# Linear attention merged with the third feed-forward: sums first in VectorE's pass, two TensorE groups moved up by one pass

## What is computed

```python
x = x + _L2_xattn_ref(_layernorm(x, axis=-1), ctx_4096, ctx_4096)
x = x + _L2_ffn_ref(_layernorm(x, axis=-1), L2_ffn_router_w, L2_ffn_A, L2_ffn_B)
...
# _L2_xattn_ref: linear attention
qh = jax.nn.softmax(qh, axis=3)
kh = jax.nn.softmax(kh, axis=1)
kvs = jnp.einsum('bnhd,bnhe->bhde', kh, vh)
out = jnp.einsum('bnhd,bhde->bnhe', qh, kvs)
# _L2_ffn_ref: top 2 of 4 experts of rank 16, gates from the logits
logits = flat @ router_w.T
topk_vals, topk_idx = jax.lax.top_k(logits, TOP_K)
gates = jax.nn.softmax(sparse, axis=-1)
mid = jnp.einsum('tf,erf->ter', flat, A)
all_deltas = jnp.einsum('ter,eor->teo', mid, B) * LORA_SCALE
delta = jnp.einsum('te,teo->to', gates, all_deltas)
```

## Time and profile before

| what | value |
|---|---|
| three runs | 1657.16, 1661.85, 5148.23 us |
| their median | 1661.85 us |
| profiled execution, time / span | 1659.5 / 1657.8 us |
| granted clock, mean of the span | 0.964 |
| busy: PE, DVE, ACT, POOL | 93%, 64%, 50%, 20% |
| the merged stage (first L929 to first L1006) | 1378.0 to 1501.5 us |

### The profile page before, as it was taken

One profiled execution on the slowest core, in us unless ns is written; L12 is line 12 of the kernel. 1 busy time (PEld: TensorE's weight loads), 2 busy tenths in 40 slices (PEclk: granted clock), 3 DMA queues, 4 the chain that ended last, 5 costly groups with the idle time before them and its releaser, 6 DMA issues.

```text
span 1657.8 us, 27915 instructions
## 1 busy us (share of the span) xinstructions
PE 1544.3 (93%) x9690; PEld 1345.1 (81%) x9690; DVE 1064.4 (64%) x2585; ACT 820.7 (50%) x2869; POOL 336.9 (20%) x353
## 2 busy tenths in 40 slices
PE   6999999999999989889999999999999997767988
PEld 5898999999999978778888888888888776655766
DVE  6566556655655687756666666666666876754664
ACT  4556445554545553355555555555555414425540
POOL 4102101110101021222222223122222213313110
PEclk9999999999999999999999999999999997868989
DMA  5101010100001001101010101010100001100001
GB/s 199 31 26 57 9 51 27 39 27 26 26 27 39 27 28 48 39 26 39 26 39 26 39 26 43 22 64 24 42 30 4 30 4 51 61 1 20 33 4 51
DMA packets 13710, 59.43 MB, mean 36 GB/s; under 512 B 2131, under 2 KB 3155, under 8 KB 8454
## 3 DMA queue, kind: packets, MB, share of 16 engines
q1 hardware_dynamic: 13574, 57.67, 9.9%
HBM read 55.57 MB, written 2.10 MB: 35 GB/s over the span
## 4 chain that ended last, share of the span: by engine, by line
PE 51%; issue 29%; DVE 11%; POOL 4%; ACT 3%; DMA 1%; POOLq 0%; SPq 0%; ACTq 0%; DVEq 0%
PE psY L772 12%; PE psQ L697 8%; PE psKV L717 7%; PE psSO L760 2%; PE psSO L666 2%; PE psQ L682 2%; POOL wo L438 2%; PE psQ L1044 1%; PE psTP L682 1%; DVE wq L1515 1%; PE psSO L667 1%; PE psTP L727 1%; PE psKV L1006 1%; PE psKV L641 1%; PE psTP L745 1%
## 5 line engine op out<-in xcount | busy, mean ns | idle before, releaser
L772 PE MATMUL psY<-wo,oT 128*128 128x512 f32 x1536 | 384.7, 399 | 1.9 <-DVE oT L1515 1.3
L772 PEld LDWEIGHTS psY<-wo,oT 128*128 128x128 f32 x1536 | 278.4, 188 | 66.0 <-POOL wo L438 2.3
L697 PE MATMUL psQ<-wq,hT 128*128 128x512 f32 x768 | 212.2, 414 | 0.3 <-DVE wq L1515 0.3
L438 POOL TENSOR_TENSOR wo<-stage_o,wo 128x512 fp32r<-128x512 f32 (+2 forms) x72 | 93.7, 1331 | 322.9 <-ACT wo L1108 322.9
L697 PEld LDWEIGHTS psQ<-wq,hT 128*128 128x128 f32 x768 | 137.9, 193 | 24.6 <-DVE wq L1515 1.2
L539 POOL TENSOR_TENSOR rms<-ms_eps,minus_half 128x5 f32<-128x5 f32 x64 | 74.7, 1167 | 390.8 <-DVE ms_eps L1678 390.8
L1177 ACT ACTIVATE prob<-s_sb,neg_mx 128x64 f32<-128x64 f32 x256 | 86.1, 337 | 110.0 <-DVE neg_mx L1665 110.0
L1180 ACT ACTIVATE prob<-wide,neg_mx 128x128 f32<-128x128 f32 x256 | 99.7, 391 | 73.7 <-DVE neg_mx L1665 73.6
L1108 ACT ACTIVATE pT<-psTP 128x512 fp32r<-128x512 f32 (+1 forms) x128 | 62.3, 486 | 131.1 <-PE psTP L745 131.1
L717 PEld LDWEIGHTS psKV<-wkv,arena 128*128 128x128 f32 x768 | 99.4, 190 | 19.8 <-DVE kT L1515 15.7
L1515 DVE TENSOR_TENSOR pT<-psTP,pT 128x512 fp32r<-128x512 f32 (+1 forms) x128 | 70.7, 552 | 65.9 <-ACT pT L1108 65.3
(11 more groups left out here) (287 smaller groups left out, 3290.4 us busy)
## 6 DMA issues: line engine op xcount, KB each, us to landing
stage_q<-in_wq SPq DMA_DIRECT2D x16, 1024.0 KB, 5.3
stage_o<-in_wo SPq DMA_DIRECT2D x16, 1024.0 KB, 4.9
stage_kv<-in_wkv SPq DMA_DIRECT2D x12, 512.0 KB, 3.6
stage_q<-in_ctx SPq DMA_DIRECT2D x16, 256.0 KB, 4.2
stage_o<-in_ctxT SPq DMA_DIRECT2D x2, 1024.0 KB, 6.9
stage_q<-in_base SPq DMA_DIRECT2D x2, 1024.0 KB, 5.1
out<-x_res SPq DMA_DIRECT2D x8, 256.0 KB, 2.0
x_res<-in_x SPq DMA_DIRECT2D x1, 1536.0 KB, 13.2
```

Source lines behind the costliest of these rows:

```text
L438: g.tensor_tensor(dst[LO], stage, dst[HI].bitcast(f32), ALU.subtract).then_inc(ld[what + "_lo"], 1)
L697: m = mm(psQ[:], lat(xl, k, n), wq[:, wl, k, :], start=k == 0 and i == 0, stop=k == KT - 1 and i == 2)
L772: m = mm(psY[:], oT[:, ol, h, :], wo[:, wl, h, :], start=h == 0 and i == 0, stop=h == HQ - 1 and i == 2)
```

## The change

Nothing is added to or taken from the computation. Tile lags stay as they are for most steps; what changes is the order within each engine's pass. On TensorE the pass is now: exponentials' transposes of t, LN-5 transposes of t-4, gate product of e, query product of t-2, key-value product of tile t (was t-1), hidden transpose of e, result transposes of t-2 (was t-3), experts of e, LN-6 transposes of e-2. On VectorE the attention sum of t-3 comes first, then `ln_lo(6, e-3)` (was e-2, at the pass's end), the key-value matrix, statistics, the exponentials' low half, and only then the experts' sum and the gates; y, `ln_lo(5)`, `hidden_lo` and the row maxima follow. ScalarE and GpSimd are reordered to match, with `ln_hi(6, e-3)` at the head of ScalarE's pass and the context's exponential and `hidden_hi` near its end. The hidden transpose moves to the gate product's bank, psS. There is one pass more, 15 in place of 14 for t (to NT + 7), which holds only the last halves of LN 6.

```diff
-    psE, psK2, psH = psSO[:, 1], psSO[:, 2, 0:2 * P], psSO[:, 2, 2 * P:3 * P]
+    psE, psK2, psH = psSO[:, 1], psSO[:, 2, 0:2 * P], psSO[:, 0, 2 * P:3 * P]
# GpSimd: ln_rstd(6, e - 1) and ln_nmr(6, e - 1, ...) moved from the head of the pass to behind q_lo
# TensorE
-            if 0 <= e < NT:
-                gate_product(f, e)
-            if 0 <= t - 1 < NT:
-                pe.wait_ge(s["eT_lo"], t)
-                need(pe, s["kvs"], t - 1)
...
-            if 0 <= t - 3 < NT:
-                u = t - 3
-                pe.wait_ge(s["y"], u + 1)
...
-            if 0 <= e < NT:
-                pe.wait_ge(s["kvs"], min(t, NT))
-                hidden_transpose(f, e)
...
                 ln_transpose(5, t - 4, free)
+            if 0 <= e < NT:
+                need(pe, FS["hidT_lo"], f.done + e)
+                gate_product(f, e)
...
                 m.then_inc(s["out"], 1)
+            if t < NT:
+                pe.wait_ge(s["eT_lo"], t + 1)
+                need(pe, s["kvs"], t)
...
+            if 0 <= e < NT:
+                hidden_transpose(f, e)
+            if 0 <= t - 2 < NT:
+                u = t - 2
+                pe.wait_ge(s["y"], u + 1)
...
             if 0 <= e < NT:
                 experts(f, e)
...
-        for t in range(3, NT + 7):
+        for t in range(3, NT + 8):
# ScalarE
-            if 0 <= e < NT:
-                gate_exp(f, e)
+            if 0 <= e - 3 < NT:
+                ln_hi(6, e - 3)
...
-            if 0 <= e < NT:
-                hidden_hi(f, e)
...
-            if t + 1 < NT:
-                ctx_exp(t + 1)
+            if 0 <= t - 4 < NT:
+                ln_hi(5, t - 4)
+            if 0 <= e < NT:
+                gate_exp(f, e)
...
-            if 0 <= e - 2 < NT:
-                ln_hi(6, e - 2)
+            if t + 1 < NT:
+                ctx_exp(t + 1)
+            if 0 <= e < NT:
+                hidden_hi(f, e)
             if 0 <= e - 1 < NT:
                 ln_norm_act(6, e - 1)
# VectorE
-            if 0 <= e - 1 < NT:
-                experts_add(f, e - 1)
-            if 0 <= e < NT:
-                gates(f, e, e - 1 if e > 0 else None, 6)
...
             if 0 <= t - 3 < NT:
                 dve.wait_ge(s["y_tr"], t - 2)
                 V.tensor_tensor(x[:, t - 3], x[:, t - 3], psY[:], ALU.add).then_inc(s["x_add"], 1)
+            if 0 <= e - 3 < NT:
+                ln_lo(6, e - 3)
...
+            if 0 <= t - 4 < NT and e < 0:
+                ln_lo(5, t - 4)
+            if 0 <= e - 1 < NT:
+                experts_add(f, e - 1)
             if 0 <= e < NT:
-                hidden_lo(f, e)
+                gates(f, e, e - 1 if e > 0 else None, 6)
...
+            if 0 <= t - 4 < NT and e >= 0:
+                ln_lo(5, t - 4)
+            if 0 <= e < NT:
+                hidden_lo(f, e)
...
-            if 0 <= t - 4 < NT:
-                ln_lo(5, t - 4)
-            if 0 <= e - 2 < NT:
-                ln_lo(6, e - 2)
```

More of the change, by code:

```diff
@@ L567, in _ @@
             e = t - 5
-            if 0 <= e - 1 < NT:
-                ln_rstd(6, e - 1)
-                ln_nmr(6, e - 1, LNS[5]["xn"])
             if 0 <= t - 1 < NT:
@@ L580, in _ @@
                 g.tensor_tensor(q_e[:, LO], q_sb[:], q_e[:, HI].bitcast(f32), ALU.subtract).then_inc(M["q_lo"], 1)
+            if 0 <= e - 1 < NT:
+                ln_rstd(6, e - 1)
+                ln_nmr(6, e - 1, LNS[5]["xn"])
             if t == 5:
@@ L954, in middle_step @@
                 m.then_inc(s["out"], 1)
+            if t < NT:
+                pe.wait_ge(s["eT_lo"], t + 1)
+                need(pe, s["kvs"], t)
+                for k in range(KT):
+                    for i, (el, cl) in enumerate(PASSES):
+                        m = mm(psK2, eT[:, el, k, :], ctxT[:, cl, k, two_tiles(t)],
+                               start=k == 0 and i == 0, stop=k == KT - 1 and i == 2)
+                m.then_inc(s["kv"], 1)
+            if 0 <= e < NT:
[3 more added lines that the diff above has]
+                pe.wait_ge(s["y"], u + 1)
+                need(pe, s["x_add"], u)
+                if u == 0:
+                    pe.wait_ge(FS["x_add"], 2 * NT)
+                for c in range(KT):
+                    i = tr(psY[:, c * P:(c + 1) * P], y_T[:, c * P:(c + 1) * P], ident[:])
+                i.then_inc(s["y_tr"], 1)
             if 0 <= e < NT:
@@ L1401, in middle_step @@
                 copy(q_e[:, HI], q_sb[:]).then_inc(s["q_hi"], 1)
-            if 0 <= t - 4 < NT:
-                ln_hi(5, t - 4)
             if 0 <= t - 3 < NT:
                 ln_norm_act(5, t - 3)
-            if 0 <= e - 2 < NT:
-                ln_hi(6, e - 2)
+            if t + 1 < NT:
+                ctx_exp(t + 1)
+            if 0 <= e < NT:
+                hidden_hi(f, e)
             if 0 <= e - 1 < NT:
@@ L1889, in middle_step @@
                 link(V.memset(logits[:, f.E:8], -3e38))
-            if 0 <= e - 1 < NT:
-                experts_add(f, e - 1)
-            if 0 <= e < NT:
-                gates(f, e, e - 1 if e > 0 else None, 6)
-            elif e == NT:
-                stats_after(f, 6, NT - 1)
             if 0 <= t - 3 < NT:
@@ L1911, in middle_step @@
                 sub_hi(eT[:, LO], slices(psE), eT[:, HI]).then_inc(s["eT_lo"], 1)
+            if 0 <= t - 4 < NT and e < 0:
+                ln_lo(5, t - 4)
+            if 0 <= e - 1 < NT:
+                experts_add(f, e - 1)
             if 0 <= e < NT:
-                hidden_lo(f, e)
+                gates(f, e, e - 1 if e > 0 else None, 6)
+            elif e == NT:
+                stats_after(f, 6, NT - 1)
             if 0 <= t - 2 < NT:
```

## The result

| | before | changed |
|---|---|---|
| median of 7 runs | 1661.19 us | 1670.58 us |
| lowest | 1657.16 us | 1665.98 us |
| profiled execution, time / span | 1659.5 / 1657.8 us | 1667.58 / 1665.9 us |
| granted clock of the span | 0.964 | 0.959 |

The ratio of the changed kernel to the one before is 1.0054, 95% interval 1.004 to 1.0069. That is 9 us more: clear of noise, and a quarter of the 2% that I gave as the bound. The forecast was 1664 in a range of 1654 to 1671, counted from the profiled execution of the kernel before (1659.5), which is 1.7 us under that kernel's median: it was a forecast of 4.6 us more. Between the two profiled executions the difference is 8.1 us.

A forecast was written before the change was run, and what follows sets the result against it. No engine is full in the merged stage; a loop of cross-engine latencies sets pass length. Early gain of 3.6 us eaten by passes 9 to 11, net +2.4, plus hand-over +2.2: +4.6 on 1659.5, 1664.1 us; range 1654 to 1671.

The forecast's parts named there:

- the 2% that I gave as the bound: Whole kernel: measured time within 2% (33 us), given 0.98.
- The loss of passes 9 to 11: LN-5 transposes wait for VectorE's LN-6 low half, gate product queued behind: 12.3 us a pass for 9.05, pass 9 13.3.
- The wait, its releaser and the norm ahead of the copy: Signs: passes 8 to 11, LN-5 transposes idle until VectorE's LN-6 hT; ScalarE's norm (0.72 us) directly before the LN-6 copy.
- The hand-over: Last experts to seventh layer's first product: 17.3 us for 15.1, +2.2, released by VectorE's arena, not GpSimd's weights.
- Passes 0 to 4: Stage start: same ring of steps cut elsewhere, no change; first experts at 1413.2, now within 0.5.
- under 2: Sign in pass 5: VectorE's two weight slices take under 2 us, 3.21 before, with most GpSimd overlap gone.
- Passes 5 to 7: a gain: VectorE runs nearly without a wait, 8.0 us a pass; 3.6 us won by experts of tile 2.
- pass 8 at full clock: Pass 8 taken at full clock, 10.4 us, the later passes at half; experts of tile 3 at 1441.8, now 1446.98.
- the loop: Chain of engine waits from one experts to the next, passes 8 to 11: 12.3 us at half clock, 9.5 at full.
- The rival in which the clock falls earlier: Gap behind the key-value product in passes 6 and 7 drops the clock: +2.6 in passes 7 and 8 each, 1669 us; chance 0.2.
- My argument against the rival (gaps of 1.19 now keep the clock): Against an earlier clock fall: kernel before has 1.19 us gaps ahead of 1427.56 and 1437.11, and the clock stays.
- its upper end: Range's top, 1671 us: takes in the earlier clock fall with the bound of the hand-over (+3).

The follow-up runs named there:

- the run with three edits: Changed kernel with gate product ahead of LN-5 transposes, LN-6 copy ahead of the norm, and tile 6's LN-6 halves back in pass 13: 1656.2 us.
- the fill alone: Changed kernel plus 8 unread identity transposes ahead of the hidden transpose in passes 6 to 9: 1666.82 us.
- GpSimd's wait alone: Changed kernel with GpSimd's low half of the queries waiting, passes 5 to 8, until VectorE has written the gated hidden tile: 1667.74 us.
- the fast version: Changed kernel with gate product, copy and sums moved first, tile 6's LN-6 halves in pass 13, and 8 unread transposes in passes 6 to 9: 1648.58 us.
- the fill and the wait: The fast version, its 8 unread transposes kept, with GpSimd's low half of the queries also waiting for VectorE's gated hidden tile: 1644.79 us.
- its run with a fill from pass 9 on: Kernel before, order untouched, plus 10 unread identity transposes ahead of the hidden transpose in passes 9 to 12: 1655.19 us.
- the fills: Changed kernel plus 8 unread transposes per place, in one run in late passes 9 to 12 (1665.17 us), in another in passes 6 to 9 (1666.82 us).
- copy first: Changed kernel with the LN-6 norm of tiles 1 to 6 moved behind the LN-6 copy on ScalarE: 1666.97 us.
- tile 6 in pass 13: Changed kernel with tile 6's LN-6 halves back in pass 13, ahead of the last norm, feature squares and weight copies: 1670.16 us.
- sums first: The run with three edits, plus VectorE's experts' sum and LN-5 statistics ahead of the LN-6 low half from pass 8 on: 1649.91 us.
- the fastest kernel: The fast version with GpSimd's wait, plus 6 unread identity transposes ahead of the hidden transpose in passes 10 to 12: 1641.54 us.

## Why the prediction came out as it did

*The loss of passes 9 to 11: right, in mechanism and size.* The forecast had 13.3, 12.3 and 12.3 us; the profile 13.5, 12.4 and 12.3, and 9.06 for pass 12 where I had 9.05. The wait, its releaser and the norm ahead of the copy are as named, and undoing the order alone took the whole loss of these passes away.

*The hand-over: right.* It takes 16.8 us, forecast 17.3, before 15.1; the seventh layer's first product waits for VectorE's arena.

*Passes 0 to 4: right, with a little luck.* The first `experts` is 0.5 us ahead of its forecast, but this profile's stage also starts 1.15 us earlier than that of the kernel before (1376.86 and 1378.01); counted from there, it comes after 35.8 us, forecast 35.2, before 35.5. The weight slices took 1.97 us, in "under 2".

*Passes 6 to 8: the step that was mis-sized.* "Passes 5 to 7: a gain" had VectorE run nearly without a wait, 8.0 us a pass, and so 3.6 us won by tile 2; "pass 8 at full clock" made it 5.2 by tile 3. Measured: 0.4 and 0.05. Each pass missed for a reason of its own.

- Pass 6 took 11.1 us in place of 10.3: the four-column gate instruction took 1.11 us beside GpSimd, 0.9 more than its 0.22.
- Pass 7 took 10.8 us in place of 8.0. The clock had fallen late in pass 6 (`experts` at 1423.79 took 1.65 us, the gate product of pass 7 2.91), and VectorE, which was to have no wait, waited 1.15 us for the exponentials and 1.50 for the gate product. With the clock up this pass took 8.07.
- Pass 8 took 12.4 us in place of 10.4, by a second fall of the clock. It had come back: `experts` at 1434.56 took 0.96 us and the LN-6 transposes 0.66. Then came 2.27 us without work, the very wait that the forecast put into the loop from this pass on, and behind it the LN-5 transposes took 1.08 and the gate product 2.91. In the run with three edits, where this wait is gone, the gate product of pass 8 took 1.66.

The rival in which the clock falls earlier was priced at +5 and given 0.2. It had pass 7 right (2.6, measured 2.8) and the sum right, but not pass 8, and it had nothing for pass 6. Its condition was the gap behind the key-value product, and that the gap is what drops the clock is shown in part only. In the changed kernel TensorE is idle 2.29 us there; the fill alone made it 1.41 and GpSimd's wait alone 1.40, and the clock fell in both. In the fast version it was 1.42 with the fill, and the clock fell; with the fill and the wait it was 0.52, and the clock stayed. But the kernel before is idle 1.89 us ahead of its hidden transpose of pass 6 and kept its clock in the profile shown; in its run with a fill from pass 9 on, whose passes 5 to 8 are the same code, TensorE is idle 3.33 us there, `experts` behind it takes 1.65 us and pass 7 11.0 in place of 9.6. My argument against the rival (gaps of 1.19 now keep the clock) compared that gap with a longer one.

So the sum was +4.6 for a measured 9, and the terms of passes 6 to 8, 5.6 us together, carry the difference. That the range held the result, by 0.4 us, is luck: its upper end was there for the earlier fall of the clock, not for what pass 6 and pass 8 did. Behind the stage, where the forecast had no change, the changed kernel's profile is 1.4 us shorter than the other (the stage ends 9.5 us later, the execution 8.1); no run explains this.

*What the order costs and what the clock does.* In the changed kernel the loop is 9.5 us at full clock and 12.3 at half by the working; the fills moved single gate products from 2.91 to 1.67 and took 4 to 5 us off the time; the order moved 9. Both together, with four further edits (copy first, tile 6 in pass 13, sums first, GpSimd's half later), made 27.

*The shared port and the clock.* The Trainium skill ("SBUF — State Buffer", Terms) has VectorE and GpSimd exclude each other on a shared port pair for a whole instruction. The trace agrees at the weight slices, to which I applied it, and at `gates`, to which I did not: VectorE's pair starts at 1413.14, 0.8 us before GpSimd's ends, and takes these 0.8 and its own 1.2; the gate instruction goes from 0.22 to 1.11 us when GpSimd's 1.29 us subtraction starts 0.2 us ahead of it, and ends with it. The Trainium skill ("TensorE: Matmul & The Clock Gate", Part 1) has the throttled clock as the default, which activity releases. The trace agrees in direction: about the same work over 55.2 us in place of 45.4 had a granted clock of 0.53 in place of 0.64.

*Open.* Why the clock fell behind 1.4 us of idle time in pass 6 of the changed kernel and not behind 1.89 in the kernel before. Why the fill in the middle passes takes 4 us off the changed kernel when its profiled execution shows a fallen clock. And what moving the key-value product and the result transposes is worth by itself, which was not tried apart from the rest.

## What to carry to other kernels

When a step that waits for another engine is moved to an earlier place in an engine's program, everything behind it inherits its wait: list what is queued there, above all the product that feeds the longest turn of the other engine. In a stage in which no engine is full, compare orders by the loop from a pass to the next, at either level of the clock, and write beside each turn what the other engines can do in it. Check every GpSimd instruction against VectorE's small ones with two SBUF inputs: 1.3 us of GpSimd can stretch 0.2 us on the critical chain.

## What the runs showed of the hardware

- A VectorE instruction of four columns, with both tensor inputs in SBUF, took 1.11 to 1.32 us while GpSimd subtracted 512 columns (1.26 to 1.29 us), in nine kernels of this family: the changed one and the eight runs on it in which GpSimd does not wait, in pass 6 of all and in pass 7 or 8 of some. It took 0.22 to 0.23 in all other passes, and in all passes of the kernel before and of the three runs with GpSimd's wait. Instructions that read PSUM beside SBUF (the division behind it, 0.69 us) kept their length while the same GpSimd instruction ran.
- Transposes of the identity that nobody reads, 6 to 10 a pass, took 0.8 to 1.3 us of TensorE time at full clock, up to 1.9 for eight at half, and could hold the granted clock at 2.4 GHz from pass 5 to 12: 1.00 in both stretches of the fastest kernel, where the same order without the late fill has 0.86 in the second.
- A fill was worth 4 to 5 us on the changed kernel and 6 on the kernel before. On the fast ones it was 1.3 to 3.5 us by medians or ratios, not clear of the intervals.
- The granted clock is not the same for the same code: in the changed kernel and its runs TensorE was idle 1.4 to 2.3 us ahead of the hidden transpose of pass 6 in ten profiles, and the clock fell in all ten: in some before `experts` of tile 1 (1.65 us), in others in it or behind it (1.31 or 0.96 us, with 2.1 to 2.5 for the gate product that follows). In the two profiles with 0.5 us there it stayed at 2.4 GHz.
